# GpSimd's gathers in a fused four-layer transformer: three more waits ahead of each chunk

## The reference

```python
# second: local attention in windows of 64 tokens, 8 heads of 64, two layers deep
sim = einsum('bhwid,bhwjd->bhwij', bq, bk)                 # scores
attn = softmax(where(mask, -max, sim))
out = einsum('bhwij,bhwjd->bhwid', attn, bv)               # probabilities times values
# third: each token gathers 33 positions of its own batch and blends neighbours
pos = base + s_idx * freq_avg + phase_avg                  # S = 33, from the tokens themselves
lo = floor(clip(pos, 0, L - 1)); hi = min(lo + 1, L - 1)
g = xh[b, lo] + frac * (xh[b, hi] - xh[b, lo])
out = silu(einsum('blshd,blhs->blhd', g, w) @ out_w.T)
```

## Time and profile before

| | |
|---|---|
| median of 3 runs | 2349.13 us |
| all runs | 2343.15, 2349.13, 2356.42 us |
| span of the profiled execution | 2353.6 us |
| its own time | not listed apart; of the three, 2356.42 lies 2.8 above the span |
| busy | PE 1720.4, PEld 1141.7, DVE 1254.1, ACT 988.0, POOL 1103.7 us |
| gathers | 1056 issues, 138.48 MB, the first at 338.1 us, the last at 2259.8 us |

### The profile page before, as it was taken

The page is one execution under the profiler, slowest core; times in us unless marked ns, Lnnn a source line. Parts: engine busy times, 40 slices in busy tenths (PEclk is TensorE's granted clock), DMA queues, the critical chain, the costliest instruction groups (busy, mean ns, idle before and its releaser), DMA issues.

```text
span 2353.6 us, 31786 instructions
## 1 busy us (share of the span) xinstructions
PE 1720.4 (73%) x12145; PEld 1141.7 (49%) x12153; DVE 1254.1 (53%) x2158; ACT 988.0 (42%) x2363; POOL 1103.7 (47%) x1069
## 2 busy tenths in 40 slices
PE   5787876767777766666776766667787768879866
PEld 3354534445445534344555434454455346656645
DVE  6565645555556444555565545655565454343345
ACT  3365673234543551243353540335354533343333
POOL 0000016475556345664556255554665367766630
PEclk8799998778989877988898978789888879989876
DMA  3010023132223232232223232232233343223321
GB/s 133 10 24 14 19 48 96 58 102 83 79 75 103 63 74 79 79 96 73 88 79 90 56 95 70 83 90 72 86 89 85 69 148 99 88 81 90 88 47 36
DMA packets 93420, 178.72 MB, mean 76 GB/s; under 512 B 21452, under 2 KB 50264, under 8 KB 93016
## 3 DMA queue, kind: packets, MB, share of 16 engines
q0 software_dynamic: 50688, 138.48, 21.4%
q1 hardware_dynamic: 42584, 38.23, 5.8%
HBM read 151.46 MB, written 9.44 MB: 68 GB/s over the span
## 4 chain that ended last, share of the span: by engine, by line
PE 39%; DVE 19%; another core or an unknown queue 18%; ACT 12%; issue 9%; SPq 1%; POOL 1%; DMA 1%; DVEq 0%; POOLq 0%; ACTq 0%
PE c L1612 5%; DVE pool_c L1235 4%; PE pa L1508 3%; PE pb L1508 3%; PE ta L1542 2%; DVE ssq L1132 2%; PE ta L1516 2%; ACT pool_a L771 2%; ACT pool_a L836 2%; PE sc L1587 2%; DVE pool_a L1155 1%; DVE pool_a L1185 1%; PE tb L1389 1%; PE pb L1560 1%
## 5 line engine op out<-in xcount | busy, mean ns | idle before, releaser
L729 POOL DMA_INDIRECT pool_c<-rows_of_x,idx x1056 | 1100.9, 1043 | 1156.5 <-PE c L1612 380.0
L1612 PE MATMUL c<-ident,pool_c 128*128 128x128 f32 x2112 | 337.1, 303 | 61.6 <-DVE pool_c L1235 32.2
L1612 PEld LDWEIGHTS c<-ident,pool_c 128*128 128x128 f32 x2112 | 278.3, 158 | 143.0 <-issue 97.0
L1235 DVE TENSOR_TENSOR pool_c<-pool_c 128x768 f32<-128x768 f32 x352 | 331.3, 951 | 20.1 <-DMA pool_c<-rows_of_x,idx 19.7
L860 ACT ACTIVATE prob<-sc,nmax 128x128 f32<-128x128 f32 x512 | 179.3, 374 | 0.1
L1516 PE MATMUL ta<-ident,pool_a 128*128 128x128 f32 x512 | 90.9, 333 | 90.8 <-DVE pool_a L1155 80.4
L771 ACT COPY pool_a<-tb 128x512 f32<-128x512 f32 x188 | 112.5, 599 | 103.6 <-remote 58.3
L1155 DVE TENSOR_TENSOR pool_a<-ta,rinv 128x512 f32<-128x512 f32 x64 | 44.3, 692 | 199.9 <-remote 158.3
L1542 PE MATMUL ta<-vmix,pool_a 128*64 128x64 f32 x1024 | 80.9, 239 | 81.0 <-ACT pool_a L771 67.5
L1142 DVE TENSOR_REDUCE nmax<-sc 128x8 f32<-128x1024 f32 x64 | 77.5, 1211 | 103.9 <-remote 96.1
L1508 PE MATMUL pa<-wqkv,pool_a 128*128 128x512 f32 x192 | 118.8, 706 | 12.9 <-DVE pool_a L1185 7.4
(11 more groups left out here) (413 smaller groups left out, 3344.3 us busy)
## 6 DMA issues: line engine op xcount, KB each, us to landing
pool_c<-rows_of_x,idx POOLq DMA_INDIRECT x1056
vmix<-vring SPq DMA_DIRECT2D x128, 128.0 KB
rows_of_x<-x2tok SPq DMA_DIRECT2D x16, 256.0 KB
xtok<-in_x SPq DMA_DIRECT2D x4, 512.0 KB
x_of_all<-x2tok SPq DMA_DIRECT2D x8, 256.0 KB
out<-pool_c SPq DMA_DIRECT2D x8, 256.0 KB, 2.3
wqkv<-in_wqkv SPq DMA_DIRECT2D x1, 1536.0 KB
xtok<-x_of_all SPq DMA_DIRECT2D x3, 512.0 KB
```

Of the source, the lines that this page charges most:

```text
L729: pool.indirect_dma_start(gat[:, n % GB, s, :], None, tables[b % 2], bass.IndirectOffsetOnAxis(ap=idx[:, t, SC * c + s:SC * c + s + 1], ax ...
L1235: V.tensor_tensor(g4, g4, wv, ALU.mult).then_inc(SEM["c_prod"], 1)
L1612: ins = mm(out[:, c:c + P], x, ident[:], start=(i == 0 and k == 0), stop=(i == BCH - 1 and k == len(parts) - 1), is_transpose=True, skip_g ...
```

## The change

GpSimd now runs through the steps of `first` too, and waits at each S and O until TensorE has finished it. Ahead of each chunk's three gathers it also waits until the three of the chunk before, in the same batch or the last of the batch before, have landed.

```diff
@@ -710,7 +710,8 @@
             def first(b, what, *a):
-                pass
+                if what in ("S", "O"):
+                    wait_filled(pool, (what, *a), b)
@@ -724,6 +725,9 @@
                 else:
                     chunk_added(pool, b - 1, CHUNKS - 1 - (CHUNKS - 1 - n) % GB)
+                prev, of = (n - 1, b) if n else (CHUNKS - 1, b - 1)
+                if of >= 0:
+                    wait(pool, f"c_gather{prev % GB}", of, 16 * SC * (prev // GB + 1))
                 t, c = divmod(n, NCH)
```

## The result

The changed kernel takes 2701.32 us (median of 4 runs, 2698.27 to 2705.14), the kernel before 2346.14 us beside it (2339.13 to 2356.42): a ratio of 1.149, 95% interval 1.145 to 1.153. The forecast was 2528, with a range up to 2630; the sign was right, the size was not.

What follows compares the result with a forecast made beforehand. No engine was simply full; gather runs held TensorE's signals. With GpSimd becoming the bound, 338.1 + 352 x 5.7 + 3 x 13.0 + 89.0 = 2472.5, plus 60 idle, less 4.5 to the median: 2528 us, range 2415 to 2630.

Steps and rivals of the forecast that it cites:

- The wait for the landing: Ahead of each chunk's gathers: a chunk takes 5.7 us, and GpSimd becomes the bound from 338.1 us on.
- Third issue to landing, 2.81: From the start of a chunk's third gather issue to the start of an engine waiting for it: 2.81 us.
- the first two steps, 2.69: GpSimd's first two issue steps in a chunk of three gathers: 2 x 1.343 = 2.69 us on average.
- the restart of a batch after its last product, 13.0: From a batch's last product to the next batch's first gather: 13.0 us, counted three times.
- I take 0.2 us for its reaction, between 0 and 0.4: GpSimd's delay in starting its next issue once the awaited gather has landed: 0.2 us per chunk.
- Lock step: Rival: VectorE and GpSimd wake together at the landing, so all chunks take 6.16 us: 2634 us, chance 0.12.
- the 60 of idle time kept apart: GpSimd idle time that stays because six buffers cannot even out the order: 60 us, some 15 a batch.
- The waits for S and O at nothing: GpSimd's waits for scores and for probabilities times values have passed by the time the old sum wait passes: 0 us.
- Relief at nothing: Shorter gather runs release TensorE's signals sooner, but TensorE spends the gain waiting for gathers: nothing in the sum.
- A third of the unknown share: Estimated shrinkage of the chain's unknown share through shorter gather runs; worth some 110 us in the bulk without GpSimd's bound.
- The two faster rivals: Relief wins with 5.0 us chunks: 2276 us, chance 0.06; both cancel with 5.3 us chunks: about 2350 us, chance 0.03.
- only the tail pays: Rival: buffers and relief hide the longer chunk except in the last batch, which costs +99: 2448 us, chance 0.18.

Runs made afterwards that it cites:

- e2: The changed kernel without the waits for scores and products (S and O), only the landing wait left: 2700.8 us, ratio 1.148 to the kernel before.
- e3: The changed kernel with an empty instruction between two waits, so the first gather itself carries the landing wait: 2662.1 us, ratio 1.133 to the kernel before.
- e1: The changed kernel without the landing wait, only the waits at S and O left: 2323.45 us, ratio 0.989 to the kernel before.
- e7: The changed kernel with half of each gathered row's bytes from the seventh chunk on: 2619.8 us, one run alone.
- e14: The changed kernel with VectorE's product on one of a chunk's three positions alone: 2674.59 us, ratio 1.162 to the kernel before.
- e4: The changed kernel waiting for the landing of chunk n-2 instead of n-1, without S and O waits: 2342.9 us, ratio 0.998 to the kernel before.
- e6: The kernel before with half of each gathered row's bytes from the seventh chunk on: 2343.7 us, ratio 0.997 to the unaltered kernel before.
- e8: The changed kernel with the landing wait only ahead of odd chunks, without S and O waits: 2338.7 us, ratio 0.996 to the kernel before.

## Why the prediction went wrong, step by step

- **The wait for the landing is what costs, and GpSimd becomes the bound: right.** e2 has the whole loss, the chain is gathers, and 292 products wait for one (forecast: well over 100). L1612's 380.0 us fell to 66.2 (forecast: under 100).
- **Third issue to landing, 2.81: right** (2.78 above), and so were the first two steps, 2.69 (2.70), and the restart of a batch after its last product, 13.0 (12.5 to 13.9).
- **"I take 0.2 us for its reaction, between 0 and 0.4": wrong, this is the step that failed.** The 0.09 us beside it is the distance of two engines that different signals had woken, so it measures no reaction, and that gather carried its wait itself; such gathers start 0.26 us after their signal. The change writes two waits, the landing's became an instruction of its own, and the gather then starts 0.71 us after VectorE. GpSimd's waits for its gathers are 2.7 us each (847.0 us in 316), not 2.1. Of the 0.63 us by which third issue to next first issue is too long (3.64 for 3.01), 0.51 are this term, the rest is mostly landings that came late. But 0.26 in its place would not have saved the forecast, as e3 shows, because of the next step.
- **Lock step at 0.12, "VectorE has other work and often comes later": wrong too, and its sign misled.** Once gathers bind, VectorE runs out of other work and starts with the landing: in 240 of 348 steps within 2.95 us of the third issue, and in 53 of the others with a landing that came later. In the 240 a chunk takes 6.17 us from third issue to third issue, where the rival had 6.16. That the rival's chunk comes out so closely is partly luck: two causes hold it at this length, and the rival named one. "First issues near 1.6 us would show lock step" did not come true (they take 1.09 on average), because the late start spends the time ahead of the issue: 0.71 + 1.07 is no other sum than 0.23 + 1.54.
- **The rest of the miss.** 348 steps x (6.34 - 5.70) = 223 us; the 60 of idle time kept apart are inside the 6.34; 163 remain, and the span came out at 2696.5 for 2532.5, 164 more. Lock step alone gave 2634; the further 62 us stand in the other 108 steps, of 6.71 us, with 3.95 us from third issue to the next first instead of 3.50. In 76 of them GpSimd's signal came more than 2.85 us after the third issue (4.14 to the next first), in 32 it did not (3.48), so late landings are the most of it; what made them late is open.
- **The waits for S and O at nothing: right here** (e2 against the change, 1.148 and 1.149), off by 1.1% for the kernel without the landing wait (e1).
- **Relief at nothing: right in effect.** "A third of the unknown share" was too careful: it went from 18% to 0%, and VectorE's two waits on remote from 254.4 to 6.0 us, but nobody on the path could use it.
- **The two faster rivals and "only the tail pays"** fell with the chunk's length: 5.36 us was the threshold, 6.34 the fact. In the last batch gathers and products cover 557 us (2051.98 to 2609.40), 40 more than the 517 forecast, the same 0.6 us a chunk less its share of the idle time.

## What to carry to other kernels

When a chain turns into wait, issue, landing, wait, read the reaction time from an instruction that waits in the same form as the new one, and ask which other engine wakes at the same signal: the engines that had other work before may have none once the new wait binds. Where two causes of the same size stand together, undoing one shows almost nothing; undo both, and each alone. In this kernel a wait meant to let a signal out had to stand ahead of the signal and had to cover both kinds that were held, or the held time only moved.

## What the runs showed of the hardware

- A GpSimd gather that carries its wait starts 0.26 us after the signal's event (e3, before); behind a separate wait instruction that had blocked it starts 0.74 us after it (the change, e7, e14). A VectorE product mostly starts 0.02 to 0.03 us after the same event, which gives the 0.23 and 0.71 between the engines. If the wait had already passed, it costs nothing (gap 0.30 us in e4).
- An issue that meets VectorE's product ends 0.82 us after the product does, whether it started 0.23 or 0.71 us into it, and whether the product took 0.96 or 0.42 us. The Trainium skill ("SBUF — State Buffer", SBUF: two separate sides) has VectorE and GpSimd share a port pair that one holds for a whole instruction, for a product with two SBUF inputs only against a GpSimd operation that reads SBUF. The trace agrees, if issuing a gather, whose row numbers (`idx`) lie in SBUF, is such an operation; no run here tests that. In the kernel before, 172 issues began inside a product (L1235) with more than 0.13 us of it left: 154 ended 0.82 us behind it, 1.41 us long on average, 9 that began within 0.03 us of its start took 0.95 us as if alone, and 9 ended later still, with further VectorE instructions in between. Those that began inside the maxima (L1142, one input, 24) and inside L1155 (one input in PSUM, 25) took 0.95 us. That the gather's last 0.82 us are what needs the pair is a reading no run here tests either.
- While GpSimd issues without a pause, many of TensorE's signals are held, though not all. In the kernel before, 831 of TensorE's instructions with a signal ended inside such a run with more than 1.5 us of it left. For 385 of them the next event of that semaphore is more than 1 us late (an event missing from the record counts as late too): for 62 of the 65 of scores (L1587) and products (L1542), but only for 92 of the 212 of sums (L1612). After the change it is 23 of 425. Half the bytes change nothing (e6). With a pause after every six issues (e8) the unknown share is 6.4% from 799 us on, for 20.6% before; with one after every three it is 0.2% of the span.
